# The slot tables of a hand-ordered transformer block on one core of Trainium2, laid anew

## The reference

```python
df = -gradv_Af + gradvv_Bf * 0.5            # layer 0: finite differences of A*f, B*f
x = jnp.maximum(f + df * dt[:, None, None], 0.0)
hidden = gelu(x @ down_W.T + down_b)        # layer 1: adapter, expert chosen by id
hidden = hidden @ Wsel + bsel + domain_emb[idx]
x = layernorm(hidden @ up_W.T + up_b + x) * ln_gamma + ln_beta
out = silu(scale * ln2d(x) + shift) @ W_in + b_in      # layer 2: FiLM
x = silu(scale * ln2d(out) + shift) @ W_out + b_out + x
x = ln(x) * (1 + scale3) + shift3           # layer 3: attention with a bias, feed-forward
scores = q @ k.T / sqrt(16) + attention_bias; scores = where(mask, -inf, scores)
x = x + softmax(scores) @ v @ Wo + bo
out = x + gelu2((ln(x) * g2 + beta2) @ W1 + b1) @ W2 + b2
```

## Time and profile before

| | us |
|---|---|
| median of 3 runs | 987.85 |
| lowest, highest | 986.80, 988.97 |
| time of the profiled execution | 987.85 |
| its span | 986.1 |
| setup, until the first L904 at 99.9 | 99.9 |
| turn 0, 99.9 to 203.0 | 103.1 |
| turns 1 to 6, each | 110.9 |
| turn 7, from 868.6, and what lies behind it | 117.5 |

### The profile page before, as it was taken

One profiled execution on the slowest core, in us unless ns is written; L12 is line 12 of the kernel. 1 busy time (PEld: TensorE's weight loads), 2 busy tenths in 40 slices (PEclk: granted clock), 3 DMA queues, 4 the chain that ended last, 5 costly groups with the idle time before them and its releaser, 6 DMA issues.

```text
span 986.1 us, 18085 instructions
## 1 busy us (share of the span) xinstructions
PE 880.4 (89%) x5643; PEld 664.7 (67%) x5731; DVE 767.8 (78%) x2375; ACT 733.8 (74%) x1901; POOL 238.9 (24%) x237
## 2 busy tenths in 40 slices
PE   7775878998999989998999989998999989999988
PEld 6354645776777767776777767776777767766766
DVE  7366787888887888888887888888888888866532
ACT  2124777978888787978888787978788787978672
POOL 2114222212242223212242223212242223111100
PEclk9667798999999999999999999999999999999999
DMA  9813554544537254544536253544537254555500
GB/s 255 226 44 86 166 157 122 146 127 120 160 111 189 81 147 132 146 128 120 159 112 189 81 148 131 147 127 120 158 110 190 81 144 134 134 132 149 165 11 22
DMA packets 133081, 130.88 MB, mean 133 GB/s; under 512 B 18265, under 2 KB 123481, under 8 KB 132969
## 3 DMA queue, kind: packets, MB, share of 16 engines
q1 hardware_dynamic: 101072, 111.49, 40.0%
q10 hardware_dynamic: 31914, 18.23, 6.6%
HBM read 112.61 MB, written 17.07 MB: 132 GB/s over the span
## 4 chain that ended last, share of the span: by engine, by line
PE 56%; DVE 18%; ACT 17%; issue 7%; DMA 1%; POOL 1%; DVEq 0%; ACTq 0%; POOLq 0%
PE ff_ps L1319 9%; PE PT_ps L1345 8%; PE G L1115 6%; PE ctx_ps L1366 6%; ACT Pr L1041 5%; PE ff_ps L1300 5%; PE scores_ps L1331 4%; DVE bias L904 3%; ACT L1041 3%; PE G L1200 3%; PE G L1123 3%; ACT PT L1054 2%; PE scores_ps L1328 2%; ACT front L990 2%; PE ff_ps L1286 2%
## 5 line engine op out<-in xcount | busy, mean ns | idle before, releaser
L1041 ACT ACTIVATE Pr<-bias,nmax 128x256 f32<-128x256 f32 x512 | 255.7, 502 | 126.0 <-DVE nmax L904 105.2
L904 DVE CUSTOM_DVE_ANT_0 bias<-scores_ps,bias 128x256 f32<-128x256 f32 x512 | 195.9, 420 | 80.2 <-issue 43.4
L1345 PE MATMUL PT_ps<-ident,Pr 128*128 128x128 f32 x1024 | 159.6, 278 | 6.9 <-ACT PT L1054 6.9
L1054 ACT ACTIVATE PT<-PT_ps 128x512 f32<-128x512 f32 x256 | 148.3, 579 | 0.2 <-PE PT_ps L1345 0.2
L1345 PEld LDWEIGHTS PT_ps<-ident,Pr 128*128 128x128 f32 x1024 | 117.6, 141 | 39.4 <-issue 28.0
L544 POOL TENSOR_TENSOR rstd<-var,half_neg 128x2 f32<-128x2 f32 (+1 forms) x64 | 40.5, 634 | 397.9 <-DVE var L669 233.2
L1300 PE MATMUL ff_ps<-ctxT,w 128*128 128x256 f32 x480 | 116.0, 384 | 7.1 <-ACT ffT L1028 6.3
L1319 PE MATMUL ff_ps<-w,ffT 128*128 128x256 f32 x480 | 112.3, 380 | 0.0
L1331 PE MATMUL scores_ps<-k_stack,q_stack 96*128 96x256 bf16 x512 | 99.1, 275 | 5.9 <-issue 1.2
L1300 PEld LDWEIGHTS ff_ps<-ctxT,w 128*128 128x128 f32 x480 | 86.4, 190 | 20.6 <-ACT ffT L1028 10.3
L1041 ACT ACTIVATION_READ_ACCUMULATOR Pr<-bias,nmax 128x1 f32 x512 | 97.5, 190 | 0.0
(11 more groups left out here) (219 smaller groups left out, 1696.7 us busy)
## 6 DMA issues: line engine op xcount, KB each, us to landing
bias<-in_fside_Bx16xSxS_dram SPq DMA_DIRECT2D x256, 256.0 KB, 3.1
part_dram<-front ACTq DMA_DIRECT2D x32, 384.0 KB, 2.7
q_stack<-part_dram SPq DMA_DIRECT2D x32, 192.0 KB, 3.4
k_stack<-part_dram SPq DMA_DIRECT2D x32, 192.0 KB, 4.1
F<-in_x_dram SPq DMA_DIRECT2D x16, 256.0 KB, 3.8
ada<-rows_dram SPq DMA_DIRECT2D x16, 256.0 KB, 5.0
q_stack<-part_dram SPq DMA_DIRECT2D x32, 128.0 KB, 3.5
k_stack<-part_dram SPq DMA_DIRECT2D x32, 128.0 KB, 4.0
```

The lines of the kernel that those rows point to most:

```text
L904: nc.vector.tensor_tensor_reduce(out=t, in0=SP_[:, n % 2, q * S:(q + 1) * S], in1=t, scale=-1.0, scalar=BIG, op0=ALU.add, op1=ALU.min, acc ...
L1041: ins = nc.scalar.activation(Pr[:, n % PR, q, :], bias[:, n // CH % RING, 2 * (n % CH) + q, :], ACT.Exp, bias=nmax[:, n, q:q + 1], scale=-1.0,
L1054: nc.scalar.activation(PT[:, m % BATCH, :, :].rearrange("p c q -> p (c q)"), TP[:, m % 2, :], ACT.Identity).then_inc(pt_ok, 1)
L1345: ins = pe.transpose(TP[:, m % 2, c * S + q * P:c * S + (q + 1) * P], Pr[:, m % PR, q, c * P:(c + 1) * P], ident[:, :])
```

## The change

The numbers in the three tables are new. No instruction is added, taken away or given to another engine. The order on SP stays as it was. The diff, cut to a few of its 28 pairs of lines; the places that they make are shown below it:

```diff
--- before.py
+++ after.py
@@ -67,36 +67,36 @@
...
-      "store": (46, 52), "prods_p": (1, 14), "prods": (1, 13), "diffs": (2, 15), "edges": (3, 15), "l0": (4, 17),
...
-      "x2": (10, 24), "stat0": (10, 25), "avg0": (11, 27), "var0": (11, 28), "inv1": (13, 30), "x2_turn": (12, 28),
...
-      "var1": (16, 32), "inv2": (15, 38), "aff1": (17, 33), "y1": (17, 33), "w_out": (19, 35), "x3": (19, 36),
-      "inv3": (18, 41), "xn3": (20, 37), "x3_turn": (23, 37), "x4T": (22, 37), "q": (24, 39), "qf": (23, 39),
...
+      "store": (51, 51), "prods_p": (1, 14), "prods": (1, 13), "diffs": (2, 15), "edges": (3, 15), "l0": (4, 17),
...
+      "x2": (10, 24), "stat0": (10, 25), "avg0": (11, 26), "var0": (11, 27), "inv1": (13, 32), "x2_turn": (12, 28),
...
+      "inv3": (27, 39), "xn3": (20, 37), "x3_turn": (21, 37), "x4T": (22, 37), "q": (24, 39), "qf": (23, 39),
...
-AT_FIRST = {"s_trig": (1, 1), "s_onehot": (2, 2), "s_grid": (1, 1), "s_h1": (1, 1), "s_h2": (5, 5), "s_h2t": (6, 6),
-            "s_sel": (2, 2), "s_cond": (10, 10), "s_condt": (11, 11), "s_mask": (23, 23), "s_rows": (16, 16),
-            "x4": (30, 44), "s_fill": (0, 0), "s_bq": (17, 17), "s_w2": (24, 24), "prods_p": (0, 12),
...
-            "avg0": (10, 24), "var0": (10, 29), "inv1": (9, 27), "x2_turn": (13, 24), "aff0": (10, 29),
...
-            "xn3": (22, 37), "x3_turn": (22, 37), "x4T": (18, 37), "q": (23, 38), "qf": (19, 38),
...
-           "store": (78, 89)}
...
+AT_FIRST = {"s_trig": (1, 1), "s_onehot": (2, 2), "s_grid": (1, 1), "s_h1": (2, 2), "s_h2": (4, 4), "s_h2t": (5, 5),
+            "s_sel": (2, 2), "s_cond": (8, 8), "s_condt": (10, 10), "s_mask": (18, 18), "s_rows": (15, 15),
+            "x4": (32, 43), "s_fill": (1, 1), "s_bq": (16, 16), "s_w2": (34, 34), "prods_p": (0, 11),
...
+            "avg0": (13, 24), "var0": (9, 28), "inv1": (8, 28), "x2_turn": (14, 28), "aff0": (10, 29),
...
+            "xn3": (17, 37), "x3_turn": (20, 37), "x4T": (20, 37), "q": (21, 38), "qf": (20, 38),
...
+           "store": (77, 78)}
```

More of the change, by code:

```diff
@@ L69 @@
 SLOTS = HEADS
-AT = {"x4": (21, 43), "ctx_spread": (16, 41), "ctx": (20, 36), "ctx_scale": (20, 36), "wo": (21, 37), "x5": (21, 38),
[1 row of a table removed]
+AT = {"x4": (30, 40), "ctx_spread": (17, 39), "ctx": (20, 36), "ctx_scale": (20, 36), "wo": (21, 37), "x5": (21, 38),
[1 row of a table added]
       "w1": ((25, 26, 28, 29), (41, 42, 43, 45)), "h1": ((25, 26, 28, 29), (41, 42, 43, 45)),
[1 row of a table removed]
-      "store": (46, 52), "prods_p": (1, 14), "prods": (1, 13), "diffs": (2, 15), "edges": (3, 15), "l0": (4, 17),
[6 rows of a table removed]
-      "q_split": (25, 40), "q_out": (25, 42), "k": (25, 40), "kf": (25, 40), "k_split": (26, 41), "k_out": (26, 41),
-      "v": (28, 45), "V": (29, 47), "mask": (20, 2)}
@@ L83 @@
-AT_FIRST = {"s_trig": (1, 1), "s_onehot": (2, 2), "s_grid": (1, 1), "s_h1": (1, 1), "s_h2": (5, 5), "s_h2t": (6, 6),
-            "s_sel": (2, 2), "s_cond": (10, 10), "s_condt": (11, 11), "s_mask": (23, 23), "s_rows": (16, 16),
-            "x4": (30, 44), "s_fill": (0, 0), "s_bq": (17, 17), "s_w2": (24, 24), "prods_p": (0, 12),
-            "prods": (1, 11), "diffs": (1, 13), "edges": (3, 14), "l0": (2, 18), "x1": (3, 21), "relu": (5, 16),
[6 rows of a table removed]
-            "q_split": (25, 40), "q_out": (24, 41), "k": (23, 40), "kf": (24, 40), "k_split": (26, 41),
-            "k_out": (24, 41), "v": (24, 45), "V": (29, 45)}
@@ L95 @@
-AT_LAST = {"ctx_spread": (15, 40), "ctx": (20, 36), "ctx_scale": (20, 38), "wo": (21, 36), "x5": (21, 39),
[3 rows of a table removed]
-           "store": (78, 89)}
[1 row of a table added]
+      "store": (51, 51), "prods_p": (1, 14), "prods": (1, 13), "diffs": (2, 15), "edges": (3, 15), "l0": (4, 17),
[6 rows of a table added]
+      "q_split": (25, 40), "q_out": (25, 42), "k": (25, 40), "kf": (25, 40), "k_split": (26, 41), "k_out": (26, 41),
+      "v": (28, 45), "V": (29, 46), "mask": (20, 2)}
+AT_FIRST = {"s_trig": (1, 1), "s_onehot": (2, 2), "s_grid": (1, 1), "s_h1": (2, 2), "s_h2": (4, 4), "s_h2t": (5, 5),
+            "s_sel": (2, 2), "s_cond": (8, 8), "s_condt": (10, 10), "s_mask": (18, 18), "s_rows": (15, 15),
+            "x4": (32, 43), "s_fill": (1, 1), "s_bq": (16, 16), "s_w2": (34, 34), "prods_p": (0, 11),
+            "prods": (2, 4), "diffs": (2, 12), "edges": (2, 13), "l0": (2, 18), "x1": (3, 17), "relu": (3, 14),
[6 rows of a table added]
+            "q_split": (26, 40), "q_out": (21, 42), "k": (23, 40), "kf": (20, 40), "k_split": (26, 41),
+            "k_out": (29, 42), "v": (28, 45), "V": (30, 45)}
@@ L100 @@
+AT_LAST = {"ctx_spread": (19, 39), "ctx": (20, 42), "ctx_scale": (20, 35), "wo": (21, 42), "x5": (21, 40),
[3 rows of a table added]
+           "store": (77, 78)}
 SP_AT = {"front": (0, 7), "stacks": (1, 2, 9, 11), "mask": 6, "rows": (12, 3)}
```

## The result

The changed kernel takes 983.98 us in the median of 8 runs (979.38 to 985.24), the kernel before 987.04 in the median of 8 (986.59 to 988.97). The ratio is 0.9958 with a 95% interval of 0.9941 to 0.9975: faster by 0.4%, 4.1 us by the ratio and 3.1 by the medians. The forecast was 984.5. The profiled execution took 983.33 us, 4.5 less than that of before, and its span is 4.6 less.

The account below looks back on a forecast made before the run. PE bounds the turns (busy 102.96 of 110.9 us); the setup is one chain between engines, often at half clock. Setup -4.0 and turns +0.7 give -3.3 from 987.85, so 984.5 us, range 980.0 to 991.0.

Parts of the forecast that it names:

- Term 1: Setup: one-hot columns no longer hold up PE's expert selection, so l0 starts at about 23.1, -4.0 us (0 to -4.0).
- Term 2: Setup: with the idle gap filled by the selection, l0 runs at full clock in about half the time, -2.8 us.
- Terms 3 and 4: Setup: s_h2 ahead of down delays the chain, +1.25 us; conditioning copy delays x2 but L746 leaves the path, +0.25.
- Term 5: Setup: stat0 of sequence 1 ahead of the splits delays q and k parts to the first score, +1.3 us.
- Term 6: Turn 0: ACT work of s_w2 ahead of the exponentials, 0 if ACT's later wait covers it, otherwise up to +2 us.
- Term 7: Turns 0 to 6: POOL's res1 slows DVE's xn3 pair by 0.7 us; leak +0.1 a turn, +0.7 in all.
- the one on the clock: Rival, chance 0.12: the clock doesn't hold under l0 in the setup, leaving -0.5 us, 987.3.
- the one on the loads: Rival, chance 0.13: loads (one-hot tables, lapT, expert matrices or stacks) set the setup as before, about 987.9 us.
- the slower one: Rival, chance 0.22: res1 beside xn3 leaks 0.7 to twice that into each of seven turns, 991.2 us.

Follow-up runs that it names:

- fill_back: The changed kernel with s_fill back in slot 0, so POOL clears V early again; ratio 0.9964 to the kernel before.
- best: The kernel before with only the changed setup table AT_FIRST, and s_w2 moved to slot 21 of the setup; ratio 0.9952 to the kernel before.
- keep_clock: The changed kernel with 24 dense 128x128 matmuls on PE between the expert selection and the first l0; ratio 0.9959 to the kernel before.
- warm_ahead: The changed kernel with 24 dense 128x128 matmuls on PE ahead of the expert selection; ratio 0.9969 to the kernel before.
- mid_only: The kernel before with only the changed table of the middle turns (AT); ratio 1.0020 to the kernel before, 988.09 us.
- last_only: The kernel before with only the changed table of the last pair's back steps (AT_LAST); ratio 0.9998, medians 987.83 and 986.81 us.
- h2_back: The changed kernel with s_h2 behind down and s_h2t behind expert again (slots 5 and 6); ratio 0.9992 to the kernel before.
- res1_back: The changed kernel with res1 of sequence 1 moved to slot 17, away from xn3; ratio 1.0090 to the kernel before, 996.95 us.
- first_only: The kernel before with only the changed table of the setup and pair 0 (AT_FIRST); ratio 0.9945 to the kernel before, 982.11 us.

## Why the prediction was right, and where it was not

The number came out within 0.6 us of the measured median, but as a sum of terms that missed in both directions. That closeness is luck: the setup gained 6.3 us by the medians of the table where 4.0 were forecast, the last turn lost 1.2 that were not, and the 0.7 lost in the middle turns did not come.

**Term 1, the one-hot columns: right.** -4.0 forecast, -3.93 measured at `l0`, -4.2 by the medians of the table; undone alone, it costs about 3 us. `lapT` is what holds `l0` now in after (2.98 us of waiting ahead of 23.17), which was named as its bound; in fill_back and best it is DVE's edge columns (L777), the other thing that `l0` waits for.

**Term 2, the clock under `l0`: wrong.** The failed step is "if the gap is filled by the selection, what remains ahead of `l0` is at most some 2.7 us without work, and `l0` at the full clock takes about half". `l0` took 5.82 us, and 5.8 to 6.3 in the seven traces of the new order; nothing was gained. Single microseconds of after, and one of fill_back behind them:

```profile
20.00:21.00 1.00, 0.19 (x2) 0.09 (x2) 0.96 (x2) 0.77 (x5) 0.00 (x0) 1.00 1.12 329
21.00:22.00 1.00, 0.00 (x0) 0.00 (x0) 0.97 (x4) 0.07 (x1) 0.00 (x0) 0.73 1.18 260
22.00:23.00 1.00, 0.00 (x0) 0.00 (x0) 0.43 (x4) 0.00 (x0) 0.00 (x0) 0.50 1.14 267
```

```profile
18.00:19.00 1.00, 1.00 (x12) 0.06 (x4) 1.00 (x3) 0.00 (x0) 0.00 (x0) 0.77 1.06 367
```

A gap of 2.98 us was left ahead of `l0`, about as forecast, and in after the clock fell in it. But the gap isn't needed. In fill_back the clock fell between 18 and 19, in keep_clock at 19.7, while PE ran the selection's thin matmuls (L1132 with 16 columns, L1151 with 33 rows) without a break; both had waited 1.3 to 1.6 us ahead of L1132. In warm_ahead, with dense matmuls in front, the clock outlasted the same selection and fell at 27.0 after 11 us without a break, the last 4.7 of them selection and `l0`. So here the selection filled the gap as far as busy time goes, and yet didn't hold the clock as dense matmuls do. The Trainium skill (TensorE: Matmul & The Clock Gate, Part 1: The HAM clock gate) speaks of idleness and of sustained work; that the clock fell under thin work, with PE busy all the time, is what these runs add. The other half of the step was nearly right: where `l0` did run at the full clock, in keep_clock, it took 3.40 us, 2.4 less than in after.

The clock did pay at another place. The `l0` of sequence 1 took 6.27 us in all three traces of the old order (63.14 to 69.41 in before) and 4.88 to 5.07 in the seven of the new (57.48 to 62.45 in after). The shorter `w_in` of after, on the other hand, is also in mid_only and last_only.

**Terms 3 and 4, `s_h2` and the conditioning: the parts right, the sum too high.** +1.5 forecast. The chain did lose 0.95 us ahead of `down` (1.25 forecast), and `x2` did come later by a wait of 1.46 us ahead of L740. But `y0` leads by 4.31 us where `x2` leads by 3.03: from `x2` to `y0` it is 9.80 us in every trace of the old order and 8.32 to 8.52 in every one of the new, so L746 left the path with its whole 1.24, not with half. From `x1` to `y0` the pair of traces gives 22.60 and 22.07 us, -0.5; the others scatter around that, 21.96 twice in the old order, 20.75 to 23.80 in the new. By the medians it is +0.1: the sum is near 0, its sign open. And h2_back shows that without the early `s_h2` the copy at L740 would have cost 3 us, so the two are one edit. The prediction priced `s_h2` as a cost of its own.

**Term 5, `stat0` ahead of the splits: not shown as sized.** +1.3 forecast. With it undone the stretch from `x1` of sequence 1 to the first score is 29.23 us, 0.15 shorter than in after and 0.8 shorter than in res1_back, the longest. In the three traces of the old order it is 29.90. So the new order as a whole costs nothing there. The kernel without it is 3.3 us faster by the ratio, and that is more than the term can explain.

**Term 6, `s_w2` in turn 0: right**, as far as 2 us can be told from 0, which was forecast; the two kernels with and without it have turn 0 at 102.3 and 102.4 us.

**Term 7, `res1` against `xn3`: right, and absorbed.** The pair was to end 0.7 us later, with 1.3 to 1.4 us for 0.73 (its own working gives 500.25 - 498.81 = 1.44). In after (line 649 in one middle turn, ns min/median/max), and in its timeline:

```profile
L649 DVE TENSOR_SCALAR front<-front,mv,rstd x2: 401/662/922, 493.1 to 493.9; 128x256 f32<-128x256 f32 x2
...
492.60 1.27 POOL L569 TENSOR_TENSOR front<-front,up_b 128x512 f32<-128x512 f32 x1
...
493.10 1.24 DVE L649 TENSOR_SCALAR front<-front,mv,rstd 128x256 f32<-128x256 f32 x2
```

One of the two operations took 922 ns beside `res1`, the other 401 behind it: +0.51. The maximum of slot 21 is 0.54 us late in every middle turn, that of slot 22 0.02 to 0.03. The leak of 0.1 a turn was none. The Trainium skill (GPSIMD Engine Reference, section 1. Specifications) names GpSimd and VectorE as sharers of SBUF interfaces, who contend when VectorE is in a 2-port mode or has two SBUF inputs. The slowdown agrees, with 922 against 401 ns, though whether L649 runs in such a mode no trace shows; and it costs nothing here.

**What the sum left out.** Two things, and a third that only looks like one.

The first is a gain. From `y0` to the `x1` of sequence 1 the old order takes 13.30 to 14.04 us, the new one 11.24 to 11.39, some 2 us less, for which the prediction had no term. 1.2 to 1.4 of it is the `l0` of sequence 1 with more of the full clock, above. The rest lies ahead of it: DVE's edge columns of sequence 1 (L771 to L777) now stand behind the statistics of `avg1`, and the step that takes up `w_in`'s result (L814) starts 3.38 us behind `y0` in after, 4.96 in before and 4.24 in mid_only. No run undid that move alone. With -4.2 at `l0`, about 0 from `x1` to `y0`, -2.0 here and -0.3 behind, the medians add up to about the 6.3 us of the setup.

The second is a loss, 1.16 us in turn 7, put down as 0 with "the last turn's feed-forward pieces keep PE as busy as before": busy it is (77.39 and 77.43), but it waits longer. Waits in about slots 23 to 31 of turn 7, in after and in best (which has the old table there), in this order:

```profile
PE ff_ps L1300 <- ACT ffT L1028: 2.3, 2, 1.5
```

```profile
PE ff_ps L1300 <- ACT ffT L1028: 0.8, 1, 0.8
```

That is 1.5 us more of wait for `ff`, against 0.6 less at L1366 (1.2 and 1.8): 0.9, which is what turn 7 loses behind slot 26. In that stretch the new table has, among others, the second piece of `w1`, the third of `h1` and the third of `ff` of sequence 0 one slot later, and `inv5` five; which of them does it was not tested.

The third is turn 0, 1.8 us longer in the pair of traces. That isn't the change, or not shown to be. The `l0` of pair 1, sequence 0, in turn 0, its first and last group of matmuls in after:

```profile
103.25 0.51 PE L1192 MATMUL G<-zeros 1*128 1x512 bf16 x1 [0.55 <-DVE front L777]
...
108.25 1.06 PE L1200 MATMUL G<-front,lapT 128*128 128x256 f32 x2
```

The same in before, and in last_only, which has the order of before up to turn 7:

```profile
110.40 0.38 PE L1192 MATMUL G<-zeros 1*128 1x512 bf16 x1
...
113.10 0.59 PE L1200 MATMUL G<-front,lapT 128*128 128x256 f32 x2
```

```profile
108.97 0.38 PE L1192 MATMUL G<-zeros 1*128 1x512 bf16 x1 [0.55 <-DVE front L777]
...
113.85 1.06 PE L1200 MATMUL G<-front,lapT 128*128 128x256 f32 x2
```

The work is the same; it takes 6.1 us in after, at half clock, 3.3 in before and 5.9 in last_only, and the scores queued behind it on PE are what DVE waits for. The table above has what follows from it: slot 4 takes 7.07 to 7.21 us where this `l0` is at half clock, 4.00 to 4.30 where it isn't, and slot 17, behind the `l0` of sequence 1, takes 2.8, 4.4 to 4.5 or 6.0. After loses 2.9 us against before at slot 4 and wins 3.2 at slot 17, with shifts of 0.6 to 1.2 us at slots 0, 6, 9 and 12 between; last_only does the same at both slots (2.8 lost, 3.2 won) with nothing changed there. Over the 14 profiled executions of this study turn 0 took between 100.8 and 106.7 us, and in four of the seven with the new order of the setup it was shorter than the 103.1 of before. That the runs of first_only and of best fall into groups with a higher and a lower mean clock fits it; that it is the whole of the scatter was not shown, since only one execution of each kernel has a trace.

Of the rivals, the one on the clock had its premise right (term 2 fell away) and its time wrong, since the setup gained elsewhere; the one on the loads had `lapT` right as the last wait ahead of `l0`, but it came 3.9 us before the old `l0`; the slower one needed a leak that didn't come.
